# Graph attention: destinations from an SBUF plane, one register load per step on SyncE and one of three numbers on VectorE

## The reference

```
xp = (x @ W).reshape(n, 2, 64)
a_src, a_dst = sum(xp * att_src), sum(xp * att_dst)         # per node and head
alpha = leaky_relu(a_src[src] + a_dst[dst], 0.2)            # per edge
m = segment_max(alpha, dst);  e = exp(alpha - m[dst])
s = segment_sum(e, dst);      w = e / (s[dst] + 1e-16)
out = segment_sum(w[:, :, None] * xp[src], dst)             # per node
```

## Time and profile before

| what | value |
|---|---|
| timed runs | 8933.91, 8934.26, 8935.12 us; median 8934.26 |
| profiled execution: span from first to last instruction | 12163.5 us |
| busy in it: GpSimd, TensorE, VectorE, ScalarE | 6376.4, 5878.0, 4437.4, 4089.9 us |
| first gather of the convolutions, of the attention | 692.1, 8738.1 us |
| mean granted TensorE clock | 0.610 of full speed |

### The profile page before, as it was taken

How to read it: one execution, slowest core, us unless ns; L and a number is a source line. 1 busy time by engine, 2 the same in 40 slices (tenths; PEclk the granted TensorE clock), 3 DMA queues, 4 the chain that set the end, 5 groups by cost and what they waited for, 6 DMA issues and landing times.

```text
span 12163.5 us, 152908 instructions
## 1 busy us (share of the span) xinstructions
PE 5878.0 (48%) x30961; PEld 4676.7 (38%) x30962; DVE 4437.4 (36%) x11587; ACT 4089.9 (34%) x12236; POOL 6376.4 (52%) x6521
## 2 busy tenths in 40 slices
PE   6844434434533444343534434343455555555555
PEld 4632322323322323232323323232355555555554
DVE  9952222222322222222312222221455555555556
ACT  6522222222322222222312222222344445445445
POOL 1656565565456565656466565656344444444443
PEclk9965555555655555555655555555566666666666
DMA  1011111111231111111211111111122222222222
GB/s 47 34 43 42 39 43 42 39 43 39 61 57 43 38 43 39 42 38 43 73 42 42 38 42 39 42 39 43 42 72 69 68 68 70 69 69 69 68 69 64
DMA packets 432692, 612.47 MB, mean 50 GB/s; under 512 B 232038, under 2 KB 249491, under 8 KB 432539
## 3 DMA queue, kind: packets, MB, share of 16 engines
q0 software_dynamic: 208832, 428.96, 13.9%
q1 hardware_dynamic: 223707, 182.02, 4.6%
HBM read 437.29 MB, written 51.28 MB: 40 GB/s over the span
## 4 chain that ended last, share of the span: by engine, by line
ACTq 30%; issue 27%; another core or an unknown queue 14%; DVE 12%; ACT 8%; PE 5%; DVEq 3%; POOL 0%; DMA 0%; SPq 0%; POOLq 0%
ACTq L893 9%; ACTq L891 9%; ACTq L906 9%; ACT g_step L906 8%; ACTq L904 2%; DVEq L1597 2%; DVE a_miss L1710 2%; ACTq L903 1%; PE bank L1190 1%; DVE a_msg L1761 1%; DVE a_max L1715 1%; DVE lo_hot L1255 1%; PE wide L1190 1%; DVE acc L1781 1%
## 5 line engine op out<-in xcount | busy, mean ns | idle before, releaser
L732 POOL DMA_INDIRECT g_rows<-gcn_table,rec_idx x4743 | 4474.9, 943 | 3125.2 <-ACT g_step L906 1707.4
L906 ACT ACTIVATE g_step<-g_rows,rec_w 128x128 f32 x5580 | 1904.4, 393 | 5800.3 <-issue 4599.8
L1190 PE MATMUL bank<-g_step,g_hot 128*128 128x128 f32 x7440 | 1750.1, 409 | 2431.0 <-ACT g_step L906 1377.0
L1190 PEld LDWEIGHTS bank<-g_step,g_hot 128*128 128x128 f32 x7440 | 1504.2, 300 | 2815.9 <-issue 2815.9
L757 POOL DMA_INDIRECT a_roll<-gat_table,src_plane x1612 | 1520.8, 943 | 1815.1 <-ACT a_cand L931 1344.2
L1627 DVE TENSOR_TENSOR acc<-acc,bank 128x512 f32 x930 | 638.3, 686 | 4137.2 <-remote 2732.6
L1190 PE MATMUL wide<-g_step,g_hot 128*128 128x128 f32 x3720 | 869.1, 407 | 1038.3 <-issue 507.0
L1225 PE MATMUL bank<-a_pair,a_hotT 128*128 128x4 f32 x3608 | 647.7, 303 | 1225.5 <-DVE a_pair L1792 1208.4
L1190 PEld LDWEIGHTS wide<-g_step,g_hot 128*128 128x128 f32 x3720 | 747.5, 299 | 1228.6 <-issue 1228.6
L1225 PEld LDWEIGHTS bank<-a_pair,a_hotT 128*128 128x128 f32 x3608 | 660.0, 273 | 1256.2 <-DVE a_pair L1792 1238.0
L931 ACT ACTIVATE a_cand<-a_miss,a_rows 128x128 f32<-128x128 bf16 x3608 | 1095.9, 386 | 39.1 <-DMA a_rows<-a_roll 27.3
(11 more groups left out here) (269 smaller groups left out, 5166.1 us busy)
## 6 DMA issues: line engine op xcount, KB each, us to landing
a_rows<-a_roll SPq DMA_DIRECT2D x451, 264.0 KB
g_rows<-gcn_table,rec_idx POOLq DMA_INDIRECT x4743
gcn_table<-rows SPq DMA_DIRECT2D x147, 256.0 KB
a_roll<-gat_table,src_plane POOLq DMA_INDIRECT x1612
e_dst<-by_dst_dst SPq DMA_DIRECT2D x451, 2.0 KB
gat_table<-acc SPq DMA_DIRECT2D x7, 462.0 KB
out_x<-xs SPq DMA_DIRECT2D x6, 448.0 KB
gcn_slots<-nothing SPq DMA_DIRECT2D x4, 468.0 KB, 6.8
```

Source lines behind the costliest of these rows:

```text
L732: pool.indirect_dma_start(out=g_rows[:, tile % RING, :], out_offset=None, in_=gcn_tables[layer % 2], in_offset=bass.IndirectOffsetOnAxis(a ...
L906: last = nc.scalar.activation(g_step[:, j, k, :].unsqueeze(1), g_rows[:, bass.ds(slots[k], 1), :], ACT.Copy, scale=rec_w[:, bass.ds(q.at(0 ...
L1190: last = nc.tensor.matmul(sums_of(j)[:, bass.ds(places[k], D)], g_hot[:, j % 3, k, :], g_step[:, j % 3, k, :], start=False, stop=(k == GP ...
```

## The change

SyncE no longer fetches destinations. All of them are loaded once, into `dst_plane` in SBUF, by 13 DMAs that stand right behind the 13 that load `src_plane`; VectorE picks a group of the plane by a register. SyncE's step then holds one load (the step less its block, from which both group and slot are taken by masks), two waits and one copy. VectorE's two loads of one number each become one load of three: the blocks of the steps q+2 and q-2 and the group of q+5, laid side by side in `gat_turn` (row 96 of the new tensor `lists`, which takes in `gcn_at`, `gat_at` and `gat_need` too). The one load stands at the head of the step, ahead of the reduction; the two stood behind it. The lists are made in nine operations of VectorE in place of five.

```diff
+LO_AHEAD = 5
+GROUP_MASK = (1 << GAT_GROUPS.bit_length()) - 1
...
-            for n in range(CSPANS):
-                sp.dma_start(planes[:, n, :, :], groups[n]).then_inc(s_src, 16)
+            for k, plane in enumerate((src_plane, dst_plane)):
...
+                for n in range(CSPANS):
+                    sp.dma_start(planes[:, n, :, :], groups[n]).then_inc(s_src[k], 16)
...
             def body(q):
-                if q.live(2):
-                    group = sp.value_load(gat_at[0:1, bass.ds(q.at(2), 1), 0], min_val=0, max_val=GAT_GROUPS - 1)
-                    if q.live(2 - R):
-                        wait_apart(sp, sa["cand"], q.at(2 - R, 1, 1), s_apart)
-                    sp.dma_start(e_dst[:, q.slot(2), :].unsqueeze(1), dst_groups[:, bass.ds(group, 1), :]
-                                 ).then_inc(s_el[q.slot(2)], 16)
                 if q.live(0):
-                    tile = sp.value_load(gat_at[0:1, bass.ds(q.at(0), 1), 0], min_val=0, max_val=GAT_GROUPS - 1)
-                    slot = sp.value_load(gat_at[0:1, bass.ds(q.at(0), 1), 1], min_val=0, max_val=ROLL - 1)
+                    _, (group,) = nc.values_load_multi_w_load_instructions(
+                        gat_at[0:1, bass.ds(q.at(0), 1)], engines=(mybir.EngineType.SP,), min_val=0,
+                        max_val=GAT_GROUPS - 1,
+                        skip_runtime_bounds_check_because="a step less its block, at most the last group")
                     if q.live(-R):
                         wait_apart(sp, sa["msg"], q.at(-R, 1, 1), s_apart)
-                    wait_apart(sp, s_land, tile + (3 * CH * CCOLS + 1), s_apart)
+                    wait_apart(sp, s_land, (group & GROUP_MASK) + (3 * CH * CCOLS + 1), s_apart)
...
-                                 a_roll[:, bass.ds(slot, 1), :, :].rearrange("p g t k -> p g (t k)")
+                                 a_roll[:, bass.ds(group & (ROLL - 1), 1), :, :].rearrange("p g t k -> p g (t k)")
...
+            gat_no = row_no[:, 0:GAT.groups]
+            for row, to in ((0, gat_at), (96, gat_turn[:, 0:GAT.groups, 2])):
+                own = gat_no[row:row + 1, :]
+                chain(V.tensor_scalar(own, gat_base[row:row + 1, :], 1.0 / P, None, ALU.mult))
+                if row:
+                    chain(V.memset(gat_turn, 0))
+                    V.tensor_copy(gat_turn[:, LO_AHEAD - 2:LO_AHEAD - 2 + GAT.groups, 0], own)
+                    chain(V.tensor_copy(gat_turn[:, LO_AHEAD + 2:LO_AHEAD + 2 + GAT.groups, 1], own))
+                chain(V.tensor_tensor(own, iota_n[row:row + 1, 0:GAT.groups], own, ALU.subtract))
+                chain(V.tensor_scalar(to, own, float(GAT_GROUPS - 1), None, ALU.min))
...
+                _, (b, b2, group) = nc.values_load_multi_w_load_instructions(
+                    gat_turn[:, bass.ds(q.at(LO_AHEAD), 1), :].rearrange("p i k -> p (i k)"),
+                    engines=(mybir.EngineType.DVE,), min_val=0, max_val=GAT_GROUPS - 1,
+                    skip_runtime_bounds_check_because="two blocks, and a step less its block")
...
-                    b, = blocks_of(gat_block[0:1, bass.ds(q.at(2), 1)])
...
-                if q.live(-2):
-                    b2, = blocks_of(gat_block[0:1, bass.ds(q.at(-2), 1)])
...
-                if q.live(5):
-                    l = q.slot(5)
-                    dve.wait_ge(s_el[l], q.landed(5))
-                    V.tensor_scalar(a_lo[:, l, :], e_dst[:, l, :],
-                                    gat_base[:, bass.ds(q.at(5), 1)], None, ALU.subtract).then_inc(sa["lo"], 1)
+                if q.live(LO_AHEAD):
+                    l = q.slot(LO_AHEAD)
+                    V.tensor_scalar(a_lo[:, l, :].unsqueeze(1), dst_of[:, bass.ds(group, 1), :],
+                                    gat_base[:, bass.ds(q.at(LO_AHEAD), 1)], None, ALU.subtract).then_inc(sa["lo"], 1)
```

More of the change, by code:

```diff
@@ L208, in gnn_kernel @@
         falls_i = sb("falls_i", [1, 1], I32)
[L209 to L212, removed]
+        lists = sb("lists", [97, ALL_GROUPS * (GP + 1)], I32)
+        gcn_at = lists[0:65, :].rearrange("p (g k) -> p g k", k=GP + 1)
+        first_at = lists[0:1, 0:ALL_GROUPS]
+        gat_at = lists[0:1, ALL_GROUPS:ALL_GROUPS + GAT.groups]
+        gat_need = lists[0:1, ALL_GROUPS + GAT.groups:ALL_GROUPS + GAT.groups + GAT_GROUPS]
+        gat_turn = lists[96:97, 0:(GAT.groups + LO_AHEAD + 2) * 3].rearrange("p (i k) -> p i k", k=3)
         gat_base = sb("gat_base", [P, GAT.groups])
@@ L311, in gnn_kernel @@
         src_plane = sb("src_plane", [P, GAT_GROUPS * GAT.tiles], I32)
+        dst_plane = sb("dst_plane", [P, GAT_GROUPS * GAT.tiles])
         gcn_scope = ExitStack()
@@ L318, in gnn_kernel @@
         listing = ExitStack()
-        row_no = sb("row_no", [65, CSTEPS], F32, listing)
+        row_no = sb("row_no", [97, CSTEPS], F32, listing)
         row_i = sb("row_i", [65, CSTEPS], I32, listing)
-        gat_group = sb("gat_group", [1, GAT.groups], F32, listing)
         listing.close()
@@ L325, in gnn_kernel @@
         T, R = GAT.tiles, GAT.ring
-        e_dst = sb("e_dst", [P, R, T])
         a_lo = sb("a_lo", [P, R, T])
@@ L387, in gnn_kernel @@
         s_gtw = sem("s_gtw")
-        s_el = [sem(f"s_el{k}") for k in range(R)]
         sa = {n: sem(f"sa_{n}") for n in ("lo", "miss", "cand", "T", "hotT", "scale", "node", "p", "msg",
@@ L394, in gnn_kernel @@
         s_ag = [sem(f"s_ag{k}") for k in range(R)]
-        s_src = sem("s_src")
+        s_src = [sem("s_src"), sem("s_src_dst")]
         s_apart = sem("s_apart")
@@ L516, in _ @@
             write_table(1, gcn_wide[1])
-            groups = by_dst[0][0:EDGES_PAD, 0].rearrange("(n g p t) -> n p g t", n=CSPANS, p=P, t=GAT.tiles)
-            planes = src_plane[:, :].rearrange("p (n g t) -> p n g t", n=CSPANS, t=GAT.tiles)
-            for n in range(CSPANS):
-                sp.dma_start(planes[:, n, :, :], groups[n]).then_inc(s_src, 16)
+            for k, plane in enumerate((src_plane, dst_plane)):
+                groups = by_dst[k][0:EDGES_PAD, 0].rearrange("(n g p t) -> n p g t", n=CSPANS, p=P, t=GAT.tiles)
+                planes = plane[:, :].rearrange("p (n g t) -> p n g t", n=CSPANS, t=GAT.tiles)
+                for n in range(CSPANS):
+                    sp.dma_start(planes[:, n, :, :], groups[n]).then_inc(s_src[k], 16)
             write_table(2, gcn_wide[0])
@@ L527, in _ @@
                              ).then_inc(s_gtw, 16)
-            dst_groups = by_dst[1][0:EDGES_PAD, 0].rearrange("(g p t) -> p g t", p=P, t=T)
             def body(q):
-                if q.live(2):
-                    group = sp.value_load(gat_at[0:1, bass.ds(q.at(2), 1), 0], min_val=0, max_val=GAT_GROUPS - 1)
-                    if q.live(2 - R):
-                        wait_apart(sp, sa["cand"], q.at(2 - R, 1, 1), s_apart)
-                    sp.dma_start(e_dst[:, q.slot(2), :].unsqueeze(1), dst_groups[:, bass.ds(group, 1), :]
-                                 ).then_inc(s_el[q.slot(2)], 16)
                 if q.live(0):
-                    tile = sp.value_load(gat_at[0:1, bass.ds(q.at(0), 1), 0], min_val=0, max_val=GAT_GROUPS - 1)
-                    slot = sp.value_load(gat_at[0:1, bass.ds(q.at(0), 1), 1], min_val=0, max_val=ROLL - 1)
+                    _, (group,) = nc.values_load_multi_w_load_instructions(
+                        gat_at[0:1, bass.ds(q.at(0), 1)], engines=(mybir.EngineType.SP,), min_val=0,
+                        max_val=GAT_GROUPS - 1,
+                        skip_runtime_bounds_check_because="a step less its block, at most the last group")
                     if q.live(-R):
                         wait_apart(sp, sa["msg"], q.at(-R, 1, 1), s_apart)
-                    wait_apart(sp, s_land, tile + (3 * CH * CCOLS + 1), s_apart)
+                    wait_apart(sp, s_land, (group & GROUP_MASK) + (3 * CH * CCOLS + 1), s_apart)
                     sp.dma_start(a_rows[:, q.slot(0), :, :].rearrange("p t k -> p (t k)").unsqueeze(1),
-                                 a_roll[:, bass.ds(slot, 1), :, :].rearrange("p g t k -> p g (t k)")
+                                 a_roll[:, bass.ds(group & (ROLL - 1), 1), :, :].rearrange("p g t k -> p g (t k)")
                                  ).then_inc(s_ag[q.slot(0)], 16)
-            run_steps(sp, GAT, R, 2, body)
+            run_steps(sp, GAT, R, 0, body)
             for c, cs in enumerate(CHUNKS):
@@ L744, in _ @@
             pool.wait_ge(s_gtw, 16 * (len(CHUNKS) + 1))
-            pool.wait_ge(s_src, 16 * CSPANS)
+            pool.wait_ge(s_src[0], 16 * CSPANS)
             def rolled(g):
@@ L1352, in plan_groups @@
                 chain(V.tensor_scalar(gat_base[:, :], bank[0][:, 0:GAT.groups], float(P), -float(P), ALU.mult, ALU.add))
-                chain(V.tensor_tensor(gat_need[:, :], iota_n[0:1, 0:GAT_GROUPS], bank[1][0:1, 0:GAT_GROUPS], ALU.add))
+                chain(V.tensor_tensor(gat_need, iota_n[0:1, 0:GAT_GROUPS], bank[1][0:1, 0:GAT_GROUPS], ALU.add))
             def code_weights():
@@ L1554, in _ @@
```

(11 more changed lines are left out.)

## The result

The changed kernel takes 9097.19 us (median of 4 runs, 9094.83 to 9098.55), the kernel before 8934.63 (4 runs). The ratio is 1.0181, 95% interval 1.0169 to 1.0193: slower by 163 us.

What follows compares the result with a forecast made beforehand. GpSimd's gather issue was taken to bound the kernel; the exposed load makes VectorE the attention's bound, 451 steps of 4.61 us, 2145 us in all against 2037. Forecast 8934 + 106 = 9040 us, range 8905 to 9130.

Steps and rivals of the forecast that it cites:

- GpSimd's issue bounds the kernel before: Nearly everywhere, GpSimd's gather issue sets the time, at 1.22 us per gather in timed runs; attention 2037 us.
- The standstills: Stretches of some 11 us with VectorE idle while GpSimd gathers: put down to the profiled execution, absent from timed runs.
- VectorE's spare time: In the attention before, VectorE needs 4.01 us per step against GpSimd's 4.36, leaving 0.35 us.
- The load ahead of the reduction: VectorE's load of three at the step's head sticks out by 0.60 us per step, bounds 0.50 and 0.79.
- the middle case: The attention with 0.60 us of VectorE's load exposed per step: 4.61 us per step, 2145 us in all.
- The sum: The attention goes from 2037 us under GpSimd to 2145 under VectorE, +108 us.
- SyncE's step, `e_dst`, the second plane, the lists at nothing: These parts of the change, in the attention and ahead of the layers, each move the time by 0 us.
- No change: Rival: GpSimd stays the bound of the attention, 8934 us within 10; chance 0.20.
- The faster rival: Timed attention runs at the pace of SyncE's and VectorE's small instructions, which the change cuts: 8836 us at 1.18; chance 0.15.
- VectorE as the bound already: Rival: VectorE bounds the attention before the change, so all of 271 us is added, about 9205; chance 0.05.
- The full price: The load sticks out by 0.79 us, or the second plane also holds up a layer: 9130, top of the main case.
- What would show it: Profile signs after: VectorE load 0.70 to 0.75 us, idle ahead of reductions, these 4.4 to 4.6 us apart behind the last gather.

Runs made afterwards that it cites:

- before_again: The kernel before, unchanged, profiled once more: 8937.45 us, profiled span 8935.7 us.
- load_behind: The changed kernel with its one load of three numbers moved behind the reduction: 8936.66 us, ratio 1.0002 to the kernel before.
- two_loads_ahead: The kernel before with its two loads of one number each moved ahead of the reduction: 9055.02 us, ratio 1.0135.
- one_number_ahead: The changed kernel with its load split, the group ahead of the reduction, the two blocks behind it: 8938.92 us, ratio 1.0005 to the kernel before.
- gather_less_before: The kernel before, GpSimd gathering only 3 of 4 tiles of each attention group from the ninth group on: 8774.46 us, ratio 0.9818.
- load_twice: The changed kernel with its load of three written twice ahead of the reduction, the unused one dropped by the build: 12271.01 us beside 12167, ratio 1.0087.

## Why the prediction was right

- **GpSimd's issue bounds the kernel before.** Shown: hardly a wait in before_again, and the time falls when only its gathers are cut. Its number was off: I took 1.22 us per gather, and it is 1.249. The 181 us that my sum had over the median, and that I spread on the gathers, lay elsewhere, for the most part between the layers: the two waits for `gcn_table`, 192.0 us in the trace that I read, are 54.9 in before_again, and from the last gather of the convolutions to the first of the attention there are 60 us (6857.7 - 6797.4) in place of 136. These two are 213 us; all the rest of that sum was some 30 us too low. The attention before was 8935.7 - 6857.7 = 2078 us, not 2037.
- **The standstills.** That they have no part in the 8934 us was right, the reason was wrong. I gave them to "the profiled execution"; but timed executions take 12167 too, and the profiles of such groups of runs have the same standstills. What sets these executions apart, no run here shows.
- **VectorE's spare time** was put at 0.35 us per step, from 4.01 against 4.36. (The eight steps of the rows give 4.00, not 4.01.) Both ends were low, by 0.09 and 0.10, and so the difference held by luck: 0.36.
- **The load ahead of the reduction.** The mechanism is shown by load_behind (all of the cost goes) and two_loads_ahead (it comes without the rest of the change). The term was mis-sized: 0.60 us, against 0.91 - 0.13 = 0.78 in an undisturbed step. In the middle case I let the whole 0.13 us from `a_lo` to the reduction hide a part of the load, and left the register operation out. Load (0.746) and register operation (0.09) are 0.83 us together, and some 0.05 of them are hidden. My bound of 0.79 was the right value for this. In the mean over all steps the load adds less, 4.82 - 4.10 = 0.72, since in some steps the reduction had to wait for something else in any case: undisturbed steps go from 3.89 to 4.67 us, by 0.78. The Trainium skill's some 200 ns per register (Runtime: NRT & Kernel Launch, Instruction fetch mechanics), given there beside the loads that the runtime adds, fits the slope of this kernel's own loads, 0.22 us per number; it has no part that comes once per load, and here that is some 0.10.
- **The sum** was +108 us (106 in the forecast). Three of its terms were off. The load adds 0.72 in place of 0.60 to the mean step: 54 us more. VectorE's own step is 4.10 in place of 4.01: 41 more. The attention before took 2078 in place of 2037: 41 less. That makes 162, and 163 were measured. The last two cancel by luck; what the forecast of 9040 lacked against 9097 is the size of the load. The 4.10 is that of the kernel before with fewer gathers, since the changed kernel with the load behind was not measured this way where the kernel before takes 8935.
- **SyncE's step, `e_dst`, the second plane, the lists at nothing.** Right: load_behind has them all and takes the time of before, and the first gather of the attention has not moved (6857.2 against 6857.7). The 13 added DMAs were issued from 2771.0 to 2805.8.
- **The rivals.** No change is what one_number_ahead gives, just at the end of the spare time; in the full change it did not occur. The faster rival needed gathers under 1.20 us and falls with 1.249. VectorE as the bound already falls with gather_less_before. The full price had the right length of the bare load, 0.79, but came to 9130: its other terms are those of my sum, and the load adds 0.72 to the mean step.
- **What would show it** in the profile was met: a load of 0.746 us, idle time ahead of the reduction, 4.51 us from reduction to reduction behind the last gather (4.4 to 4.6 was the sign), SyncE's longer wait for `a_msg`, and gathers every 1.25 us wherever GpSimd does not wait.

## What to carry to other kernels

A register load costs the sequencer by the numbers it loads (0.22 us each here, and 0.10 once), so joining loads saves little by itself; what counts is which running instruction it lies under. Put loads behind the issue of the longest operation of a step, not at the step's head. Compare what sticks out with the spare time of that engine, which is found by leaving out a part of the bounding engine's work and seeing where the time stops. Before a profile is trusted for shares, compare its span with the timed runs, and profile again if they differ.

## What the hardware showed unexpectedly

The same kernel took 8935 us in some groups of runs and 12167 in others, each repeatable within 0.4%. The chip's number does not decide it: runs on the one numbered 0 gave 12167 and, 20 minutes later, 8935. GpSimd's gathers take 0.94 us each in both. In the profile of 12163.5 us VectorE stands still for up to 15 us in the attention's steady part (24 in the convolutions), and VectorE, ScalarE and TensorE all at once for up to 13, while gathers are issued. Beside 12167 the changed kernel (as load_twice, which comes to the same instructions) costs 104 us (ratio 1.0087) and not 163. And there a slower step of VectorE can go with a faster kernel: with a quarter of the attention's gathers left out, the kernel with the exposed load is faster by 264 us than the one with the hidden load (11045 against 11310). That the density of GpSimd's gathers couples the two is a guess that fits; it was not tested, and the cause is open.

That a load whose registers are not read is dropped by the build is no matter of the hardware, but it voids an experiment that doubles a cost. Count the instructions in the profile first.
